# Neighbour sums of a graph layer: 16 of 49 destination tiles by gathered rows instead of by counts

## The reference

```python
xn = _layernorm(x)
# 206250 edges (src, dst), sorted by dst: each node has itself and random neighbours, 33 edges in the mean
agg = segment_sum(xn[src], dst, num_segments=6250)
x = x + relu(((1 + eps) * xn + agg) @ W1 + b1) @ W2 + b2 + linear_attention(xn)
x = x + bidirectional_sums(lstm(_layernorm(x)))      # one sequence of 6250 in windows of 50 steps
```

## Time and profile before

| | us |
|---|---|
| median of 3 runs | 2207.38 (2206.28 to 2210.11) |
| the profiled execution | 2208.27 |
| its span, first to last instruction | 2206.4 |
| TensorE busy in the span | 1947.5 (88%) |
| VectorE | 1600.4 (73%) |
| ScalarE | 1183.9 (54%) |
| GpSimd | 197.6 (9%) |

### The profile page before, as it was taken

How to read it: one execution, slowest core, us unless ns; L and a number is a source line. 1 busy time by engine, 2 the same in 40 slices (tenths; PEclk the granted TensorE clock), 3 DMA queues, 4 the chain that set the end, 5 groups by cost and what they waited for, 6 DMA issues and landing times.

```text
span 2206.4 us, 42629 instructions
## 1 busy us (share of the span) xinstructions
PE 1947.5 (88%) x13254; PEld 1550.7 (70%) x13254; DVE 1600.4 (73%) x4208; ACT 1183.9 (54%) x3147; POOL 197.6 (9%) x274
## 2 busy tenths in 40 slices
PE   5678998999999999999999989997679998899845
PEld 4467885666666666666668868886468887888833
DVE  7876887777777777777746967777876666566687
ACT  4465444554554554554533446666875665566527
POOL 3343001000000000000002200000000000000060
PEclk8799998999999999999999999997569999899975
DMA  4222221010010010010015302223443333233403
GB/s 121 93 66 83 96 94 34 25 31 29 24 31 29 24 31 29 24 31 28 24 31 176 99 38 111 111 111 130 167 140 99 126 122 113 85 122 123 122 2 116
DMA packets 96636, 170.48 MB, mean 77 GB/s; under 512 B 8053, under 2 KB 68681, under 8 KB 96224
## 3 DMA queue, kind: packets, MB, share of 16 engines
q1 hardware_dynamic: 67693, 86.80, 12.1%
q10 hardware_dynamic: 27088, 77.11, 10.9%
q0 software_dynamic: 1744, 5.21, 0.8%
HBM read 110.53 MB, written 58.56 MB: 77 GB/s over the span
## 4 chain that ended last, share of the span: by engine, by line
PE 58%; DVE 20%; ACT 10%; issue 7%; DMA 2%; POOL 2%; DVEq 0%; ACTq 0%; POOLq 0%; SPq 0%
PE psum L663 27%; PE psum L812 10%; PE psum L658 7%; PE psum L769 4%; ACT scr L1113 2%; DVE scr L1495 2%; DVE scr L1704 2%; ACT scr L1121 2%; DVE bufB L1621 1%; DVE bufB L1706 1%; DVE scr L1702 1%; PE psum L846 1%; ACT scr L1080 1%; DVE bufA L1822 1%; PE psum L607 1%
## 5 line engine op out<-in xcount | busy, mean ns | idle before, releaser
L663 PE MATMUL psum<-halves,counts 128*128 128x512 f32 x2401 | 759.8, 423 | 16.2 <-ACT counts L1018 16.2
L1520 DVE TENSOR_TENSOR wx<-rs_buf 128x392 bf16<-128x392 bf16 (+1 forms) x1568 | 545.6, 391 | 211.6 <-PE psum L658 207.9
L1018 ACT ACTIVATE counts<-psum 128x392 fp32r<-128x392 f32 x784 | 390.3, 498 | 359.1 <-PE psum L658 357.7
L812 PE MATMUL psum<-bufB,wx 128*128 128x125 f32 x3392 | 425.5, 284 | 32.5 <-DVE bufB L1706 21.3
L812 PEld LDWEIGHTS psum<-bufB,wx 128*128 128x128 f32 x3392 | 401.3, 194 | 56.7 <-DVE bufB L1706 38.4
L663 PEld LDWEIGHTS psum<-halves,counts 128*128 128x128 f32 x2401 | 393.7, 189 | 65.9 <-ACT counts L1018 21.8
L658 PEld LDWEIGHTS psum<-wx 128*128 128x128 bf16 x3136 | 170.8, 99 | 199.0 <-issue 192.0
L658 PE MATMUL psum<-wx 128*128 128x98 bf16 x3136 | 284.8, 213 | 4.0 <-DVE wx L1520 2.9
L769 PE MATMUL psum<-bufA,wx 128*128 (+1 forms) x800 | 181.7, 379 | 3.2 <-POOL rs_buf L524 3.2
L769 PEld LDWEIGHTS psum<-bufA,wx 128*128 128x128 f32 x800 | 147.9, 190 | 20.7 <-issue 3.4
L1121 ACT ACTIVATE scr<-scr 128x125 f32<-128x125 f32 x280 | 86.1, 307 | 121.1 <-DVE scr L1704 115.8
(11 more groups left out here) (262 smaller groups left out, 2530.6 us busy)
## 6 DMA issues: line engine op xcount, KB each, us to landing
bufA<-gates_of_x ACTq DMA_DIRECT2D x136, 500.0 KB, 3.4
gates_of_x<-bufB SPq DMA_DIRECT2D x24, 1000.0 KB, 3.9
x_times_eps_plus_sums<-scr SPq DMA_DIRECT2D x50, 128.0 KB, 1.7
sums_by_feature<-scr SPq DMA_DIRECT2D x50, 128.0 KB, 1.9
scr<-x_times_eps_plus_sums SPq DMA_DIRECT2D x49, 128.0 KB, 2.0
wx<-in_x_dram SPq DMA_DIRECT2D x25, 250.0 KB
x_plus_mix<-wx SPq DMA_DIRECT2D x25, 250.0 KB, 4.5
bufB<-x_plus_mix SPq DMA_DIRECT2D x25, 250.0 KB, 2.6
```

The lines of the kernel that those rows point to most:

```text
L663: return mm(psum[:, 3 + v, :], cnt[v][:, hi, :], xhl[:, hi, :, :].rearrange("p s d -> p (s d)"), start=(hi == 0), stop=(hi == NT - 1))
L812: return mm(gate_half(u, m, gate), whhv[:, k, (2 * gate + m) * P:(2 * gate + m + 1) * P], h, start=False, stop=(k == 1), skip_group_check= ...
L1018: fn(cnt[v][:, :, c * u:c * (u + 1)], psum[:, CB[u % 4], 0:PER * KEYS].rearrange("p (c h) -> p h c", h=NT), ACT.Copy).then_inc(S["c_sb"], 1)
L1520: last = tt(to, tab2[:, 0:k_, :].unsqueeze(1).broadcast_to([P, PER // 2, k_, 2]), keysT[v][:, part_, g0:g0 + PER // 2, :].unsqueeze(2).bro ...
```

## The change

NC=33 destination tiles stay with counts, the NG=16 others are made from rows of x. x in its two parts is stored in DRAM once (`xt_d`, 12.8 MB), and the two edge lists are copied there with a margin. A gathered tile has RUN=35 times 128 consecutive edges from its first one on: partition p holds 35 sources and 35 destinations. For each of the 35 GpSimd gathers 128 rows of 2 KB by an indirect DMA into one of XB=7 buffers, VectorE compares the destinations with 0 to 127 (five of the 35 in one operation of 128x640, two buffers), and TensorE multiplies one-hot and rows (`add_rows`) into PSUM bank 6. Edges of other tiles compare with nothing and add zero.

The loop runs 8 times over four counted tiles and two gathered ones. The 35 products of a gathered tile are put behind the counting products of the units 3 to 31 of two counted tiles, one or two a unit (`slot`). GpSimd waits for the products that free the buffers before the gathers 0, 2 and 4 of each seven, and behind gather 14 it issues two index gathers for the next tile (`run_of`). The small operation before the key gather becomes a semaphore increment. The rows of a gathered tile are added, turned and stored as those of a counted one; TURNS becomes NT+2. The buffers of the rows lie over weights and scratch of the query stage, so the gathers start when it is over. At the end of a pass GpSimd takes the semaphores of the gathers back down. Semaphores of other stages are merged, and some buffers move in `rs_buf`. The diff, cut to its core:

```diff
-STEP_UNITS = NT * UNITS
-TURNS = NT + 1
-EVEN, ODD = (NT + 1) // 2, NT // 2
+NC = 33
+NG = NT - NC
+NCB = -(-NC // STEPS_PER_BLOCK)
+RUN = 35
+HOT = 5
+XB = 7
+FIRST_SLOT = 3
+STEP_UNITS = NC * UNITS
+TURNS = NT + 2
+EVEN, ODD = (TURNS + 1) // 2, TURNS // 2
...
+        def slot(w):
+
+            return FIRST_SLOT + w * (2 * UNITS - FIRST_SLOT) // RUN
...
+    xt_d = nc.dram_tensor("x_in_two_parts", (NT * P, 2 * D), F32R).ap()
+    run_src = nc.dram_tensor("sources", (E + 64,), I32).ap()
+    run_dst = nc.dram_tensor("destinations", (E + 64,), I32).ap()
...
+                    for to, of in ((run_src, src), (run_dst, dst)):
+                        pool.dma_start(to[0:E].rearrange("(p e) -> p e", p=66), of.rearrange("(p e) -> p e", p=66)).then_inc(S["tab_st"], 16)
+                        pool.dma_start(to[E:E + 64].rearrange("(p e) -> p e", p=1), no_edge[:, :]).then_inc(S["tab_st"], 16)
...
-                pool.wait_ge(S["gat_t"], count + 1)
                 pool.wait_ge(S["gat_a"], count + 1)
-                pool.tensor_tensor(tick[0:1, 0:1], ones[0:1, 0:1], ones[0:1, 0:1], ALU.add).then_inc(S["gat_t"], 1)
+                pool.sem_inc(S["gat_t"], 1)
...
+            def run_of(v):
+
+                for to, of in ((src_run[v], run_src), (dst_run[v], run_dst)):
+                    pool.indirect_dma_start(out=to[:, :], out_offset=None, in_=of.rearrange("(e o) -> e o", o=1),
+                                            in_offset=bass.IndirectOffsetOnAxis(ap=run_i[:, v:v + 1], axis=0)).then_inc(S["run_ld"], 16)
...
+            pool.wait_ge(S["hi_act"], NT)
+            pool.wait_ge(S["lo_q"], NT)
+            for q in range(XCH):
+                t0, t1 = tiles(q)[0], tiles(q)[-1] + 1
+                pool.dma_start(xt_d[t0 * P:t1 * P, :].rearrange("(t p) d -> p t d", p=P),
+                               xhl[:, t0:t1, :, :].rearrange("p t s d -> p t (s d)")).then_inc(S["tab_st"], 16)
+            pool.wait_ge(S["tab_st"], 16 * (XCH + 4))
+            run_of(0)
+            pool.wait_ge(S["pj_ps"], NB)
             with pool.Fori(0, n) as k:
-                with pool.Fori(0, NGB // 2) as i:
-                    b0 = pool.snap(k * NGB + 2 * i + 2)
+                with pool.Fori(0, NG // 2) as i:
+                    b0 = pool.snap(k * NCB + 2 * i + 2)
                     for c in range(2):
                         gather(pool.snap(b0 + c), c)
-                gather(pool.snap(k * NGB + (NGB + 1)), 0)
-            pool.wait_ge(S["gat_t"], n * NGB + 3)
-            pool.wait_ge(S["gat0"], n * (16 * (NGB + 1) // 2) + 16)
-            pool.wait_ge(S["gat1"], n * (16 * (NGB // 2)) + 16)
-            pool.tensor_tensor(tick[0:1, 0:1], ones[0:1, 0:1], ones[0:1, 0:1], ALU.add).then_inc(S["gat_t"], 1)
+                        gq = pool.snap(k * NG + 2 * i + c)
+                        pool.wait_ge(S["run_ld"], i * 64 + (32 * c + 32))
+                        pool.sem_inc(S["gat_t"], 1)
+                        done = pool.snap(gq * RUN)
+                        for w in range(RUN):
+                            if w % XB in (0, 2, 4):
+                                pool.wait_ge(S["m_mm"], done + (NT - XB + 1 + w + (2 if w % XB == 4 else 1)))
+                                pool.sem_inc(S["gat_t"], 1)
+                            pool.indirect_dma_start(out=rows_g[w % XB], out_offset=None, in_=xt_d,
+                                                    in_offset=bass.IndirectOffsetOnAxis(ap=src_run[c][:, w:w + 1], axis=0)
+                                                    ).then_inc(row_gat[w % XB], 16)
+                            if w == 2 * XB:
+                                pool.wait_ge(S["m_mm"], done + NT)
+                                pool.wait_ge(S["edge_v"], gq * 2 + 17)
+                                pool.sem_inc(S["gat_t"], 1)
+                                run_of(1 - c)
+                gather(pool.snap(k * NCB + (NCB + 1)), 0)
+                pool.wait_ge(S["m_mm"], k * (RUN * NG) + (NT + RUN * NG))
+                pool.wait_ge(S["edge_v"], k * (2 * NG) + (16 + 2 * NG))
+                pool.sem_inc(S["gat_t"], 1)
+                pool.wait_ge(S["run_ld"], 32 * NG + 32)
+                pool.inc_swdge_sem([S["run_ld"]] + row_gat, [32 * NG] + [16 * NG * RUN // XB] * XB, mode="sub")
+                pool.sem_inc(S["settled"], 1)
...
+            def add_rows(landed, hots, c, w):
+
+                pe.wait_ge(row_gat[w % XB], landed + 16 * (w // XB + 1))
+                if w % HOT == 0:
+                    pe.wait_ge(S["oh_v"], hots + (4 + w // HOT))
+                mm(psum[:, 6, :], oh_d[(c + w // HOT) % 2][:, w % HOT, :], rows_g[w % XB],
+                   start=(w == 0), stop=(w == RUN - 1)).then_inc(S["m_mm"], 1)
...
+                with pe.Fori(0, NC // BODY) as i:
+                    q0 = pe.snap(k * TURNS + i * 6)
                     u0 = pe.snap(k * STEP_UNITS + i * (BODY * UNITS))
-                    b0 = pe.snap(k * NGB + 2 * i)
+                    b0 = pe.snap(k * NCB + 2 * i)
                     for j in range(BODY):
-                        v = j % 2
+                        v, c = j % 2, j // 2
+                        if v == 0:
+                            landed = pe.snap(i * (32 * RUN // XB) + c * (16 * RUN // XB))
+                            hots = pe.snap(k * (RUN // HOT * NG) + i * (2 * RUN // HOT) + c * (RUN // HOT))
                         pe.wait_ge(S["c_sb"], u0 + (UNITS * (j + 1) + len(CB)))
-                        pe.wait_ge(S["row_v"], q0 + (j + 1))
+                        pe.wait_ge(S["row_v"], q0 + (3 * c + 1 + 2 * v))
                         hi = 0
                         for u in range(UNITS):
                             for _ in range(3):
                                 multiply(v, hi)
                                 hi += 1
-                            if j % 2 == 0 and u == 4:
-                                turn_keys(pe.snap(b0 + (1 + j // 2)))
-                            if u == 10:
-                                turn_rows(pe.snap(q0 + j), 1 - v)
+                            if v == 0 and u == 4:
+                                turn_keys(pe.snap(b0 + (1 + c)), pe.snap(q0 + 3 * c))
+                            for m, at in ((3 * c, 6), (3 * c + 1, 12), (3 * c + 2, 10 + UNITS)):
+                                if at == v * UNITS + u:
+                                    turn_rows(pe.snap(q0 + m), 1 - m % 2, pe.snap(b0 + (1 + c)))
                             count(pe.snap(u0 + (UNITS * (j + 1) + u)), u)
+                            for w in range(RUN):
+                                if slot(w) == v * UNITS + u:
+                                    if w == 0:
+                                        pe.wait_ge(S["row_v"], q0 + (3 * c + 2))
+                                    add_rows(landed, hots, c, w)
...
+            def dst_of(loaded, c, ahead, base):
+
+                dve.wait_ge(S["run_ld"], loaded)
+                ts(run_i[:, 1 - c:2 - c], ahead, float(E), None, ALU.min).then_inc(S["edge_v"], 1)
+                ts(dst_here[c][:, :], dst_run[c][:, :], base, None, ALU.subtract).then_inc(S["edge_v"], 1)
+
+            def dst_hot(multiplied, converted, c, m):
+
+                dve.wait_ge(S["m_mm"], multiplied)
+                if m == 0:
+                    dve.wait_ge(S["edge_v"], converted)
+                tt(oh_d[(c + m) % 2], dst_here[c][:, HOT * m:HOT * (m + 1)].unsqueeze(2).broadcast_to([P, HOT, P]),
+                   tab[:, :].unsqueeze(1).broadcast_to([P, HOT, P]), ALU.is_equal).then_inc(S["oh_v"], 1)
...
+                            c2 = j // 2
+                            if j % 2 == 0 and u == 0:
+                                dst_of(dve.snap(i * 64 + (32 * c2 + 32)), c2,
+                                       run_f[:, ds(2 * i + (c2 + 1), 1)], tile_0[:, ds(2 * i + c2, 1)])
+                            if j % 2 == 0 and u == FIRST_SLOT:
+                                row_sums(dve.snap(q0 + 3 * c2), 6, done + (NT + RUN * c2), 1 - 3 * c2 % 2, ld + (1 + 16 * ((3 * c2 + 1) // 2)))
                             if u == RING:
-                                row_sums(dve.snap(q0 + j), s0 + (j + 2), 1 - j % 2, ld[1 - j % 2] + (1 + 16 * ((j + 1) // 2)))
+                                m = 3 * c2 + 1 + j % 2
+                                row_sums(dve.snap(q0 + m), 4 - j % 2, s0 + (j + 2), 1 - m % 2, ld + (1 + 16 * ((m + 1) // 2)))
+                            for m in range(RUN // HOT):
+                                if slot(HOT * m) - 1 == j % 2 * UNITS + u:
+                                    dst_hot(dve.snap(done + (NT + RUN * c2 + HOT * (m - 1))), dve.snap(gq * 2 + (18 + 2 * c2)) if m == 0 else 0, c2, m)
```

More of the change, by code:

```diff
@@ L127, in build @@
         wih, whh = wx[:, 0:2 * G4], wx[:, 2 * G4:4 * G4]
+        with nc.sbuf_tensor("over_w", [P, 8 * D], F32R) as over_w:
+            pass
         wq, wk, wv, wp = (sb(n, 2 * D) for n in ("wq", "wk", "wv", "wp"))
@@ L259, in build @@
         ld_x = [sem(f"ld_x{v}") for v in range(XR)]
```

(10 more changed lines are left out.)

278 lines of the change are left out of this document (169 added, 109 removed).

## The result

The kernel after takes 2385.83 us in the median of 4 runs (2378.37 to 2387.24), the kernel before 2206.97 beside it (2206.28 to 2210.11): a ratio of 1.080, 95% interval 1.078 to 1.083. The forecast was 2110 us and faster. The profiled execution has a span of 2385.4 us, 179.0 more than before.

What follows compares the result with a forecast made beforehand. TensorE was taken to bound the neighbour sums: 16 groups at 43.2 us instead of 49.58 give -102.1, plus 5 of extras, -97 us, so 2110 us. The range was 2065 to 2180, the case's own 2084 to 2145.

Steps and rivals of the forecast that it cites:

- TensorE's cost of a group: Two counted tiles and one gathered in the new loop: 41.35 us of TensorE, 40.8 as the lower figure.
- VectorE's: VectorE's work in a group of the new loop: 29.2 us of 41, hidden behind TensorE.
- ScalarE's: ScalarE's copies in a group of the new loop: 17.5 us, hidden behind TensorE.
- GpSimd's cost: 38 gather issues a group at 1.05 us: 39.9 us, just under TensorE's 41.35; bounds 36.7 and 45.0.
- the overlap: GpSimd's gathers beside TensorE in a group, nearly as long as TensorE's own work; no cost added for lying beside it.
- What is late next: Mid-tile index gathers delay row gathers; TensorE loses 1.9 us once a group, making 43.2.
- rival of the ring: Seven row buffers decide once landing reaches 5.3 us; at 6.5 us no gain, 2211 us; chance 0.13.
- the dear gather: Gathering 2 KB rows costs twice that of 1 KB rows: 70.5 us a group, 2546 us, slower; chance 0.13.
- slower: Outcome that the whole kernel becomes slower than before: chance 0.17.
- The DMA engines' cost: Row gathers at 0.94 us of all engines and rows in and out: 36.9 us a group, about 90% busy.
- The rest: Store of x, list copies, last turn and new steps outside the groups: 5 us together, bounds 0 and 17.
- signs of being wrong: A group under 40.8 or over 45 us, or the stage before the loop growing by over 12 us.

Runs made afterwards that it cites:

- e1: Changed kernel without its 560 row gathers and their waits, products reading rows already in SBUF: 667.0 us from first to last product by counts, against 961.7.
- e11: Changed kernel without row gathers and with 22 more TensorE signals a group: 666.8 us from first to last product by counts.
- e14: Changed kernel with a plain 256 KB GpSimd load in place of each row gather, same waits: 684.8 us from first to last product by counts.
- e13: Changed kernel with 26 of a group's 35 row gathers kept, products reading SBUF: 785.8 us from first to last product by counts.
- e3: Changed kernel with GpSimd waiting before each gather for the product freeing its buffer, instead of three times in seven: 2402.64 us.
- e4: Changed kernel with gathered rows of 1 KB instead of 2 KB: 959.3 us from first to last product by counts, against 961.7.
- e6: Changed kernel with gathers of 16 rows instead of 128, products reading SBUF: 976.2 us from first to last product by counts, against 961.7.
- e18: e17's kernel with the store of x spread over the query stage, each piece waiting for two more blocks: 2160.93 us, ratio 0.979 to the kernel before.
- e17: Changed kernel with a gathered tile behind five counted ones instead of two, nothing left out: 2174.17 us, ratio 0.985 to the kernel before.
- e2: Changed kernel with all gathers issued but no product waiting for them, GpSimd mostly waiting for its own older gathers: 1308.9 us from first to last product by counts.
- e5: Changed kernel with a GpSimd addition of two 128x256 float32 tiles in place of each row gather: 774.3 us from first to last product by counts.
- e9: Changed kernel with TensorE signalling 15 gathered products a group instead of 35: 4450.01 us, a run that can't be used.
- e15: The kernel of e9 run again, 15 signalled gathered products a group instead of 35: 2390.08 us.

## Why the prediction was wrong

Two steps of it failed, and together they cost 16.1 us a group (59.3 for 43.2): the cost of a gather's issue, 4.1 of them, and the overlap, 12.0.

- *TensorE's cost of a group*, 41.35 and 40.8 from below: right, 40.8 in e1 and e11. *VectorE's* and *ScalarE's*: right (29.65, 17.55), the 128x640 one-hots took 0.825 us against 0.82.
- **The first step that failed is GpSimd's cost**, "I take 1.05 a gather ... 39.9, just under TensorE's 41.35". Issues without a wait follow each other at 1.244 us, 0.94 busy and 0.30 before the next:

```profile
361.19 0.94 POOL L559 DMA_INDIRECT over_s<-x_in_two_parts,src_run  x1 [0.30 <-issue]
362.43 0.94 POOL L559 DMA_INDIRECT over_s<-x_in_two_parts,src_run  x1 [0.30 <-issue]
363.67 0.94 POOL L559 DMA_INDIRECT over_s<-x_in_two_parts,src_run  x1 [0.30 <-issue]
```

  38 of them are 47.3 us, above TensorE's time and above my upper bound of 45.0. The earlier trace rows had only 0.15 us between a small operation and a gather, no two gathers in a row, and I filled that hole with plain issues, which do follow without idle time, as in e14 too. That alone would have made 47.3 a group, and even with the 23 us at the start the change 13 us faster (16x2.3 less 23).
- **The second and larger is the overlap.** The other 12.0 us a group stand in no term of mine: "the work put beside TensorE is thus nearly as long as TensorE's own", and for lying beside it I priced it at nothing, without a reason. It makes the others learn late what TensorE has done. TensorE then idles (187.5 us of the stretch, 2.8 in e1) and, at the lower clock and with products that no longer overlap, is busy 110 us longer; how these 110 divide is not shown. The mis-sized pace isn't what brought this on: the 39.9 us forecast are 96% of 41.35, and at e13's 88% an issue already cost 0.26 us.
- *What is late next*: TensorE waited for rows 89.3 us in 800 (waits of 400 to 1200 us, L758 on over_s 46.8 and over_w 42.5), 6.6 a group and not 1.9. But GpSimd had itself waited 114.4 us for gathered products in this time (82.5 and 31.9 in the rows above), so late signals also made it ask late; how much of the 6.6 us comes from that is not shown. The rival of the ring is wrong by e3, that of the dear gather by e4 and e6: 0.94 us for 2 KB rows as for 1 KB. For this rival the prediction named a rule of the Trainium skill ("DMA: Bandwidth & Descriptors", SWDGE vs HWDGE vs iDMA: a float32r destination always casts). e14 has the same destination, takes GpSimd 0.567 us an issue and loses 1.1 us a group, so the change failed beside this rule, not by it. The 0.17 that I gave to "slower" were for this rival and the ring; that it came out slower is no merit of theirs.
- *The DMA engines' cost*, 0.94 us of all 16 for a row gather: about right. From 500 to 1200 us that queue has 110.04 MB in 64.0%, which is 1.07 us for 262 KB. The 0.60 that I estimated from the Trainium skill ("DMA: Bandwidth & Descriptors", Anatomy of one DMA: bytes over 436e9 a second) is too low for this transfer. The queue's row (packets, MB, share):

```profile
q0 software_dynamic: 60674, 110.04, 64.0%
```

- *The rest*, 5 us, bounds 0 and 17: it was 23. The store, put at 2 us, costs 17.7 by e18 beside e17 (13.2 in their medians, 10 to 18 with the spread of the first product); some 7 us of the 23 remain that no run explains. I had set its 40 us against engines that are 70% idle in the mean; but all ten pieces were issued in 8.7 us, the DMA share from 193 to 250 us was 0.94, and the stage's loads stood behind them.
- Of the sum: 155 of the 179 us are 16x(59.3 - 49.58), 23 the start, 1 the rest. Two of the signs of being wrong that I had named came true, a group over 45 and a stage before the loop that grows by over 12.

## What to carry over

Price a stream of gathers on GpSimd by issue, 1.24 us each whatever its rows, and keep it under two thirds of GpSimd's time, in short rows with pauses between, where other engines live on TensorE's signals: the same scheme lost 8% at 116% and won 1.5% at 54%. Work beside the engine that bounds the kernel isn't free just because it is shorter. A profile in which no engine is full and the longest waits are many times the operation waited for is a sign that signals are late; look at what another engine does at these moments. A large store that has time is to be issued in pieces, paced by the stage that it lies beside.

## What was not expected of the hardware

- The lateness: TensorE's counts reach ScalarE up to 7.9 us late beside gathers by index, while ScalarE's and VectorE's own signals are on time. Late ones are recorded 0.12 us apart (609.07 to 609.42). With gathers that wait for no product, TensorE itself stalls by 1.9 to 2.6 us between products, signalling or not (e2). It follows neither bytes, rows, traffic nor the number of signals. By what path GpSimd's work reaches TensorE no run here shows. One rival stays untested: beside gathers the trace also lacks records of signals (458 of 512 counts and 349 of 512 copies are there, all 768 of each before), so the recording may have a part in it, and no time here is of an execution without it.
- GpSimd adding in SBUF slows VectorE from 0.34 to 0.55 us an instruction in the mean (e1, e5), its 128x392 one-hots from 0.353 to 0.709; gathers do so hardly (143.19 us for 413 in the same window of the kernel after, 0.35).
- The waiting goes with a lower clock: granted 0.91 from 600 to 900 us against 1.00 in e1, products at the 1.2 GHz level after a stall (three in 1.48 us at 603.97, 0.85 otherwise), and 516.4 us for the 1617 products by counts against 472.2 in e1.
- In e9's run the products by counts took 782 ns in the median for 397, and products were slow from the first stage on. Its trace shows a granted clock of 1.00, but holds no record of the clock at all, and 782 is near what such a product takes at the 1.2 GHz level in other runs (796 at most). So the 1.00 is no reading; that TensorE ran at the lower level throughout fits, but is not shown. e15 ran the same kernel normally.
